# ScalarE writes the planes of the first layer later in its order, and joins read planes before it splits turned rows

## The reference

```python
x = L0_attn_data                                     # (4, 1024, 1024)
x = _layernorm(x + _L0_attn_ref(x, ...), axis=-1)    # first:  x @ (weight * block mask).T
x = _layernorm(x + _L0_ffn_ref(x, ...), axis=-1)     # second: x @ W.T + bias + a LoRA adapter chosen per batch
x = _layernorm(x + _L1_attn_ref(x, ...), axis=-1)    # third:  project to 128, 4 blocks (scan + MLP), project back
x = _layernorm(x + _L1_ffn_ref(x, ...), axis=-1)     # fourth: x @ W.T + b + routed LoRA experts
```

## Time and profile before

| | |
|---|---|
| median of 3 timed runs | 1688.17 us (1686.18 to 1688.62) |
| the profiled execution | 1684.57 us, its span 1682.3 us |
| mean granted TensorE clock | 0.986 |
| PE busy | 1619.8 us (96%) |
| DVE, ACT, POOL busy | 1135.3, 809.0, 432.4 us |
| first layer's pairs | about 98 to 315 us |
| tiles 27 to 31 | about 315 to 382 us |
| second layer | about 382 to 840 us |

### The profile page before, as it was taken

How to read it: one execution, slowest core, us unless ns; L and a number is a source line. 1 busy time by engine, 2 the same in 40 slices (tenths; PEclk the granted TensorE clock), 3 DMA queues, 4 the chain that set the end, 5 groups by cost and what they waited for, 6 DMA issues and landing times.

```text
span 1682.3 us, 22807 instructions
## 1 busy us (share of the span) xinstructions
PE 1619.8 (96%) x7734; PEld 1301.1 (77%) x7734; DVE 1135.3 (67%) x2150; ACT 809.0 (48%) x1115; POOL 432.4 (26%) x379
## 2 busy tenths in 40 slices
PE   8999998899999999999899999999899999999998
PEld 7877777677888888888776676676678788888886
DVE  6777766455565656566777777777958776776633
ACT  3766655566555545544445455555533333333311
POOL 4100000120000000001376777773223222221200
PEclk9999999999999999999989999999999999999999
DMA  7233322454444444452140000002546555655321
GB/s 276 91 110 116 120 76 97 151 142 119 119 116 120 118 117 116 113 157 75 51 173 26 1 1 1 1 1 90 182 170 222 164 208 192 196 193 182 132 88 50
DMA packets 140195, 196.58 MB, mean 117 GB/s; under 512 B 75954, under 2 KB 84146, under 8 KB 139826
## 3 DMA queue, kind: packets, MB, share of 16 engines
q1 hardware_dynamic: 115250, 125.92, 25.5%
q10 hardware_dynamic: 24832, 69.22, 10.6%
HBM read 105.97 MB, written 72.35 MB: 106 GB/s over the span
## 4 chain that ended last, share of the span: by engine, by line
PE 75%; DVE 8%; issue 6%; ACT 6%; DMA 3%; POOL 2%; ACTq 0%; SPq 0%; POOLq 0%; DVEq 0%
PE ps L880 13%; PE ps L882 13%; PE ps L881 13%; PE ps L1126 6%; PE ps L1068 3%; PE ps L959 2%; PE ps L961 2%; PE ps L960 2%; ACT planes_early L1424 2%; PE ps L1074 2%; DMA x_scratch<-planes_early 2%; PE ps L1026 2%; PE ps L1118 2%; PE ps L1116 2%; PE ps L1117 2%
## 5 line engine op out<-in xcount | busy, mean ns | idle before, releaser
L880 PE MATMUL ps<-wall_x,x_hi 128*128 128x512 f32 x688 | 275.3, 400 | 8.3 <-ACT wall_x L1488 3.0
L2639 POOL TENSOR_TENSOR rstd<-var_eps,minus_half 128x1 f32<-128x1 f32 x96 | 65.8, 686 | 830.6 <-DVE minus_mean L1925 830.6
L882 PE MATMUL ps<-wall_x,x_lo 128*128 128x512 f32 x688 | 270.2, 393 | 0.0
L881 PE MATMUL ps<-wall_x,x_hi 128*128 128x512 f32 x688 | 269.9, 392 | 0.0
L880 PE MATMUL ps<-wall_y,x_hi 128*128 128x512 f32 x512 | 202.2, 395 | 0.0
L881 PE MATMUL ps<-wall_y,x_hi 128*128 128x512 f32 x512 | 199.6, 390 | 0.0
L882 PE MATMUL ps<-wall_y,x_lo 128*128 128x512 f32 x512 | 199.6, 390 | 0.0
L880 PEld LDWEIGHTS ps<-wall_x,x_hi 128*128 128x128 f32 x688 | 130.4, 190 | 38.2 <-ACT wall_x L1488 5.2
L882 PEld LDWEIGHTS ps<-wall_x,x_lo 128*128 128x128 f32 x688 | 130.1, 189 | 28.0
L881 PEld LDWEIGHTS ps<-wall_x,x_hi 128*128 128x128 f32 x688 | 130.6, 190 | 25.4
L1857 DVE TENSOR_TENSOR row<-ps,bias 128x512 f32<-128x512 f32 x128 | 87.8, 686 | 86.2 <-PE ps L882 84.8
(11 more groups left out here) (329 smaller groups left out, 3623.3 us busy)
## 6 DMA issues: line engine op xcount, KB each, us to landing
x_scratch<-row ACTq DMA_DIRECT2D x32, 512.0 KB, 3.1
x_in<-x_scratch SPq DMA_DIRECT2D x32, 512.0 KB, 4.1
out<-row ACTq DMA_DIRECT2D x32, 512.0 KB, 2.7
x_in<-in_x_t SPq DMA_DIRECT2D x29, 512.0 KB, 3.7
w_first<-in_w_t SPq DMA_DIRECT2D x56, 256.0 KB, 2.9
x_scratch<-planes_early ACTq DMA_DIRECT2D x27, 512.0 KB, 3.2
cx<-x_scratch SPq DMA_DIRECT2D x24, 512.0 KB, 4.3
x_scratch<-cx ACTq DMA_DIRECT2D x24, 512.0 KB, 3.9
```

Source lines behind the costliest of these rows:

```text
L880: pe.matmul(bank, hi[:, k], wall[:, k, 0, cols], start=(k == 0), stop=False)
L881: pe.matmul(bank, hi[:, k], wall[:, k, 1, cols], start=False, stop=False)
L882: return pe.matmul(bank, lo[:, k], wall[:, k, 0, cols], start=False, stop=(k == KC - 1))
L2639: pool.tensor_tensor(rstd[:, i:i + 1], var_eps[:, i:i + 1], minus_half[:, 0:1], ALU.pow)\
```

## The change

`part_planes` of the pair's second tile (`a - 1`) moves behind `hold(p, 1)` and the two `op_hi` (or `take_b`) after it. `take_a(0)` moves ahead of the last pair's normalise and planes. In tiles 27 to 31 `part_planes` moves from the weight parts to behind the evacuation of half 0. At tile 32 the last planes move behind both weight parts. In the whole second layer `join_planes(s + 2)` moves from the end of the iteration to ahead of SiLU, square and `split_y`. No instruction is added or taken out; only ScalarE's order differs, its DMA issues with it.

```diff
@@ pairs
-                part_planes(a - 1)
                 hold(p, 1)
                 if more:
                     op_hi(p + 1, S2)
                     op_hi(p + 1, S3)
                 else:
                     take_b(0, 0)
+                part_planes(a - 1)
                 hold(p, 2)
@@ after the pairs
+            take_a(0)
             normalise(S_END - 2)
             part_planes(S_END - 2)
-            take_a(0)
             for s in range(S_END, A_END):
...
                     if i == 1:
                         normalise(s - 1)
-                    if i == 2:
-                        part_planes(s - 1)
                 evacuate(s, 0)
+                part_planes(s - 1)
                 if s == S_END + 1:
                     split_a()
                 evacuate(s, 1)
@@ second layer
                 normalise(s - 1)
-                if s == A_END:
-                    part_planes(s - 1)
                 if more:
                     weight_hi(n)
                 if i % 2 and i >= 3:
                     evacuate_h((i - 3) // 2)
                 if more:
                     weight_hi(n + 1)
+                if s == A_END:
+                    part_planes(s - 1)
+                if s + 2 < B_END:
+                    join_planes(s + 2)
                 if s > B_END - EARLY:
                     silu_x(s - 1 - B_END + EARLY)
                 if s >= B_END - EARLY:
                     square1(s - B_END + EARLY)
                 if i >= 1:
                     split_y(s - 1)
-                if s + 2 < B_END:
-                    join_planes(s + 2)
```

## The result

| | before | after |
|---|---|---|
| median, timed side by side | 1686.18 us (7 runs, 1681.84 to 1688.62) | 1677.11 us (7 runs, 1674.45 to 1679.29) |
| span of the profiled execution | 1682.3 us | 1674.4 us |
| mean granted clock | 0.986 | 0.986 |
| PE, DVE, ACT, POOL busy | 1619.8, 1135.3, 809.0, 432.4 us | 1622.7, 1131.0, 806.4, 454.6 us |

The ratio is 0.9945, with a 95% interval of 0.9932 to 0.9958: 9.1 us faster, where 13.1 were forecast. The time lies in the range of 1666 to 1686 and near its middle, but not every term does.

The account below looks back on a forecast made before the run. TensorE, 96% busy, was taken as the bound, its waits in the pairs due to planes ahead of `hold(p, 1)`. The terms -24.4 + 1.7 + 3.4 + 6.2 = -13.1 us gave 1675.1 from 1688.2, range 1666 to 1686.

Parts of the forecast that it names:

- Pairs, what goes: Pairs, 98 to 315 us: 20.4 us of TensorE waits and 6 of half clock go, 26.4 together.
- Pairs, what comes: Pairs: late sums delay `hold(p, 2)` and VectorE's join, so A22 waits; 2 us (0 to 5) over four pairs.
- The room of 0.8: Pairs: VectorE's join frees A22's bank at 171.6, while A22 would start at 172.4.
- Tiles 27 to 33: Stretch behind the pairs: gains and losses from moving `take_a(0)` and planes, net +1.7 us.
- tile 28: Planes now stand between two evacuations, so high part, weight sum and TensorE at 346.24 come 2.2 us later (0 to 2.5).
- First three batches: Second layer: joins first make `y_hi`, `y_lo` and half 1's row 2.43 later; +3.4 us (0 to 14).
- a room of 0.2: First three batches, tiles with a projection: `y_lo` ends at 423.42, wanted at 423.63, so no loss.
- Last batch: Second layer's end: joins delay rows and squares, +1.5 in tiles 57 and 59, +0.8 in 60, +2.4 in 61; +6.2 us.
- rival E: Clock falls in tile 62 too and stays low longer around 58 and 60, +2.6 each; 1678 to 1683 us, chance 0.18.
- A: Whole kernel: the forecast itself, 1675 us, from 1670 to 1680; chance 0.48.
- the rule: Tile 62: idle gaps throttle the array, so it would start slow, some 13 steps, 2.6 us; left out of the sum.
- Its own signs: Wrong if pairs keep waits above 5 us total, or second layer (382 to 840) takes under 5 or over 16 more.

Follow-up runs that it names:

- The runs alone: Kernel before with one edit: planes of a pair's second tile behind `hold(p, 1)`; 1662.05 us against 1685.06, ratio 0.9861.
- with few columns: Kernel before, order untouched, ScalarE copying only 64 of 1024 columns of each plane for tiles 6 to 25, stores full size; 1660.80 us, ratio 0.9857.
- the last run with matmuls: Changed kernel plus matmuls of 128 columns in two waits, 14 in tile 60 and 17 behind tile 61; 1679.32 us, ratio 0.9960.
- Filling the waits: Extra matmuls in TensorE's last-batch waits: changed kernel 1675.76 us, resized 1679.32; without joins ahead 1664.36; with planes directly behind `hold(p, 1)` too 1660.84.

## Why the prediction came out as it did

**Pairs, what goes: right.** The forecast removed 26.4 us. The shift is 22.7 and the new waits take about 3.9, so 26.6 went. The runs alone (-23.0) and with few columns name the reason as the prediction did.

**Pairs, what comes: right place, half the size.** 2 us were given to late sums. Three waits at A22 cost 1.06 to 1.09 each beyond a normal step, and S1 still started 0.4 late in the second pair; with small ones this is 3.9. The room of 0.8 was enough in the other pairs; late sums were forecast for four pairs and came in three. Moving the planes ahead of the sums' high parts removed the waits, which shows the cause.

**Tiles 27 to 33: right in sum, wrong in one step.** Tile 27 gained 0.3 (forecast 0.5) with the wait of 1.78 where it was expected. The picks of 381.28 gained 1.45 and lost 0.67 to a new wait for `b_rows`; tile 33 lost 1.3 (forecast 1.4). The step that failed is tile 28: 2.2 us were forecast and the wait grew from 0.46 to 0.57. The prediction took the planes to fill a wait for a weight sum. That sum ended at 339.61 before, which a shift of -23.56 puts at 316.05, and after at 314.00: it was there 2 us sooner, so the planes only changed places with work of the same length. One of the 2 us is the load ahead of the sum, the other the instruction that waits for it (1.35 before, 0.29 after). VectorE before, then VectorE and ScalarE in tile 28 of the changed kernel:

```profile
337.53 1.35 DVE L1947 TENSOR_TENSOR w_more<-w_more,ident 128x128 f32<-128x128 f32 x1 [1.99 <-DMA w_more<-in_w_t]
```

```profile
312.98 0.29 DVE L1946 TENSOR_TENSOR w_more<-w_more,ident 128x128 f32<-128x128 f32 x1 [1.00 <-DMA w_more<-in_w_t]
314.03 0.63 ACT L1488 ACTIVATE wall_y<-w_more 128x512 fp32r<-128x512 f32 x1
314.57 0.58 ACT L1399 ACTIVATE row<-ps 128x512 f32<-128x512 f32 x1
315.05 1.99 ACT L1424 ACTIVATE planes_late<-row 128x1024 uint16<-128x1024 uint16 x2
```

The forecast term itself is real where the sum is late. With the planes directly behind the middle held block the load came as late as before (a wait of 2.03, 311.51 above), and TensorE waited 2.60 where it had waited 0.46: 2.1 us, for 2.2. So the mechanism was right, and the load that it was read from was late in the trace of before and in that run alone, of fourteen traces; in the last run with matmuls it was half as late and cost 0.9. In the term's place came 1.2 us of half clock behind the wait at 349.04, which stood in the kernel before without it. The sum of the stretch is partly luck: over the ten traces with the new order here it cost between 0.2 and 7.1 us.

**First three batches: the mechanism right, 1.6 too small.** Nine even tiles lose 0.3 to 0.4, 2.9 to 3.2 together as the edges are drawn (forecast 2.7). Six tiles with a projection lose about 0.2 each, 1.1 to 1.3, where the prediction saw a room of 0.2 and charged nothing: a wait without any visible idle time still costs a slower start.

**Last batch: mis-sized most, +10.8 for 6.9.** The named places cost 0.72, 1.52, 1.55, 1.01 and 2.73, 7.5 together, against 0.65, 1.5, 1.5, 0.8 and 2.4. Half 1 of tile 57 (+0.6) was missed. The last 2.6 are half clock behind the longer waits, rival E, which had 0.18: about 1.0 in tile 58 and 2.4 behind tile 61, while in tile 60 before lost as much. It came with A, not instead of it. The prediction had left this out because the next wait would swallow most; the wait for `rstd` at 809.05 gave back 0.9 of the 2.4.

The Trainium skill ("TensorE: Matmul & The Clock Gate", section "HAM oscillation — how this bites in real kernels") has a kernel in which each wait for a transfer throttles the array and the next burst starts cold. After 4.29 us of waiting tile 62 did (800.55). It was right to weigh the rule, and in this trace its price was missing from the sum. Filling the waits won nothing and putting the joins back won 15 to 18 us, so it is the longer waits that must go. What a full clock alone would be worth behind tile 61 stays open.

**Its own signs: one failed.** The waits left in the pairs are 3.0 us in total, under the 5 named. But the second layer, from 382 to 840 us, takes 17.2 us more (shift -23.89 to -6.71), above the 16 that the prediction called its limit. Without tiles 32 and 33, which the sum counts with the stretch before, it is 15.1, for the 9.6 of the sum. The total fell inside the range because the other stretches were near and the range was wide.

The last 1.2 us, behind 845 us, are no effect of the change. They are one wait of the trace before:

```profile
1228.54 0.47 PE L880 MATMUL ps<-wall_x,x_hi 128*128 128x512 f32 x1 [0.90 <-ACT wall_x L1488]
```

The step to this matmul is 1.29 there and 0.23 in all thirteen other traces, while the order around it is the same in all of them. So it belongs to that one execution.

## What to carry over

When a fast engine waits for a copy, look what stands ahead of that copy in its engine's order and move it into a wait of the same engine, not just behind the copy: behind `hold(p, 1)` the planes gained 23 us, placed in ScalarE's own wait for the sums perhaps a little more, one step too far they lost 10. A swap inside a chain that ends 0.2 us before its deadline is no small matter: it gave back two thirds, 4.3 us in 24 tiles that lose 0.2 to 0.4 at a time, and 10.8 in the last batch, where TensorE already waited for that chain. A single trace can hold a load or a wait that the next execution doesn't have, so a term that hangs on one late transfer needs a second look. Edits that are put together for one aim should be timed apart, since here one alone is worth 1.4% and the other costs 0.9%.

## What the hardware showed that was not expected

The same wait does not always bring the clock down. Half 1 of tile 60 waited 2.06 us in both of these kernels; with the pairs alone:

```profile
759.90 0.50 PE L880 MATMUL ps<-wall_x,x_hi 128*128 128x512 f32 x1 [2.06 <-DVE row L1857]
760.24 0.57 PE L881 MATMUL ps<-wall_x,x_hi 128*128 128x512 f32 x1
760.61 0.63 PE L882 MATMUL ps<-wall_x,x_lo 128*128 128x512 f32 x1
```

and without the joins ahead:

```profile
758.12 0.50 PE L880 MATMUL ps<-wall_x,x_hi 128*128 128x512 f32 x1 [2.06 <-DVE row L1856]
758.46 0.39 PE L881 MATMUL ps<-wall_x,x_hi 128*128 128x512 f32 x1
758.69 0.39 PE L882 MATMUL ps<-wall_x,x_lo 128*128 128x512 f32 x1
```

The first runs seven steps at 1.2 GHz, the second stays at 2.4. So one trace of such a stretch can be off by 1.4 us for each wait. Before, seven steps were slow behind 2.07 us at the same place. Another place shows the same: the weight part of tile 27 (298.19 above) waited 1.78 or 1.79 us in ten traces, and seven slow steps followed in five of them, none in the other five. A f32 matmul of 128 columns is recorded as two instructions of 0.12 us: 14 of them are 28 records and 3.29 us (765.08 above).
